# Four transposes, the weights and the outputs share three PSUM banks; the norm's guard moves in front of the logarithm

## The reference, cut to what matters

```python
def l2norm(t):
    return t / jnp.maximum(jnp.linalg.norm(t, axis=-1, keepdims=True), 1e-12)
...
q = l2norm(q) * qs
k = l2norm(k) * ksc
q = q * cos * scale + rotate_half(q) * sin * scale
k = k * cos * inv + rotate_half(k) * sin * inv
out = local_attention(q, k, v)          # each window sees itself and the window before it
return out.reshape(b, n, INNER) @ Wo
...
for i in range(DEPTH):                  # DEPTH = 6
    x = attn_layer(shift_tokens(x), ...) + x
    x = ffn_layer(shift_tokens(x), ...) + x
```

## Time and profile before

| | |
|---|---|
| median of 3 runs | 4022.69 us (4015.24 to 4051.56) |
| the profiled execution | 4047.98 us, its span 4046.1 us |
| busy in the span | PE 3125.7 us (77%), DVE 2893.7 (72%), ACT 2117.6 (52%), POOL 1116.3 (28%) |
| stretch of the six layers, 1847 to 4046 us | PE 1731.61, DVE 1592.81, ACT 1237.02, POOL 1031.53 us busy |
| mean TensorE clock granted there | 0.98 |
| stretch ahead of it, 0 to 1793 us | PE 1379.29, DVE 1271.36, ACT 871.76 us busy |

### The profile page before, as it was taken

How to read it: one execution, slowest core, us unless ns; L and a number is a source line. 1 busy time by engine, 2 the same in 40 slices (tenths; PEclk the granted TensorE clock), 3 DMA queues, 4 the chain that set the end, 5 groups by cost and what they waited for, 6 DMA issues and landing times. The chain is left out here.

```text
span 4046.1 us, 67071 instructions
## 1 busy us (share of the span) xinstructions
PE 3125.7 (77%) x25619; PEld 1597.3 (39%) x25853; DVE 2893.7 (72%) x4198; ACT 2117.6 (52%) x3147; POOL 1116.3 (28%) x627
## 2 busy tenths in 40 slices
PE   3899999994433888966777777777877777777887
PEld 1122222221321333324554555355545535554554
DVE  4888888875742788846775777677677767776775
ACT  2366666664221455654664565465556646654664
POOL 2000000000020000015553555355345535553551
PEclk7799999997666999988999999999999999999999
DMA  3200000000023000001111101000110011110100
GB/s 93 37 1 1 1 1 1 1 1 6 0 72 46 2 1 1 1 33 41 30 30 34 33 27 45 26 27 28 39 33 28 27 34 34 32 44 22 32 27 22
DMA packets 56649, 100.33 MB, mean 25 GB/s; under 512 B 19782, under 2 KB 38148, under 8 KB 54916
## 3 DMA queue, kind: packets, MB, share of 16 engines
q1 hardware_dynamic: 56324, 95.92, 9.2%
HBM read 37.95 MB, written 7.34 MB: 11 GB/s over the span
## 5 line engine op out<-in xcount | busy, mean ns | idle before, releaser
L456 DVE TENSOR_REDUCE a_part<-ps 128x1 f32<-128x512 f32 (+3 forms) x1664 | 1010.9, 656 | 343.3 <-PE ps L330 310.4
L440 ACT ACTIVATE a_Pb<-ps 128x1024 f32<-128x1024 f32 (+3 forms) x832 | 778.3, 973 | 640.6 <-PE ps L406 634.2
L1013 PE MATMUL ps<-l_w_qkv,l_XS 128*128 128x512 f32 x1152 | 586.0, 632 | 206.8 <-DVE l_weights L1403 163.0
L330 PE MATMUL ps<-a_KS,a_QS 128*128 128x512 bf16 (+3 forms) x1592 | 567.5, 385 | 102.4 <-DMA a_QS<-pieces 44.3
L956 POOL TENSOR_TENSOR l_sine<-l_qn,l_tab 128x512 f32<-128x512 f32 x192 | 341.4, 1778 | 776.8 <-DVE l_qn L1375 776.7
L406 PE MATMUL ps<-a_QS,a_KS 128*128 128x512 bf16 (+3 forms) x1598 | 466.9, 368 | 19.6 <-DVE a_part L456 7.1
L1362 DVE TENSOR_REDUCE l_norm<-l_square 128x8 f32<-128x512 f32 x384 | 262.0, 686 | 298.1 <-ACT l_square L1217 286.7
L383 PE MATMUL ps<-a_Pb,V 128*32 128x512 f32 (+3 forms) x3328 | 422.8, 580 | 2.6 <-ACT a_Pb L440 1.3
L330 PEld LDWEIGHTS ps<-a_KS,a_QS 128*128 128x128 bf16 x1664 | 145.2, 98 | 649.7 <-DVE a_part L456 573.1
L1024 PE MATMUL ps<-ident,l_hat 128*128 128x128 f32 x1536 | 252.0, 288 | 150.9 <-ACT l_kT L1241 67.2
L1013 PEld LDWEIGHTS ps<-l_w_qkv,l_XS 128*128 128x128 f32 x1152 | 206.5, 199 | 383.3 <-DVE l_weights L1403 175.5
(11 more groups left out here) (184 smaller groups left out, 4605.5 us busy)
## 6 DMA issues: line engine op xcount, KB each, us to landing
l_V_earlier<-l_V SPq DMA_DIRECT2D x96, 384.0 KB, 3.5
l_V_earlier<-l_V SPq DMA_DIRECT2D x96, 128.0 KB, 3.4
l_w_qkv<-in_L_ffn_Wqkv_dram SPq DMA_DIRECT2D x6, 1536.0 KB, 8.2
pieces<-a_piece SPq DMA_DIRECT2D x12, 512.0 KB, 2.6
a_KS<-pieces SPq DMA_DIRECT2D x48, 128.0 KB
a_QS<-pieces SPq DMA_DIRECT2D x48, 128.0 KB
l_w_o<-in_L_ffn_Wo_dram SPq DMA_DIRECT2D x6, 512.0 KB, 3.9
a_cos<-in_c_cos_dram SPq DMA_DIRECT2D x2, 1024.0 KB, 5.4
```

The source lines that it names most:

```text
L330: mm = e.matmul(bank[:, 0:width], QS[:, c, head, qt * P:(qt + 1) * P], KS[:, head, b * CH:b * CH + width], start=not masked, stop=True, sk ...
L440: e.activation(Pb[:, n % 2, 2 * p:2 * p + 2, a:CH], ps[:, 2 * p:2 * p + 2, a:CH], ACT.Exp)\
L456: e.tensor_reduce(part[:, u % 2, h * TC + qt, b:b + 1], ps[:, 4 + n % 2, 0:width], AX.X, ALU.max)\
L1013: e.matmul(ps[:, (V_BANK[T] if i == 2 else 0) + b, :], XS[:, T * P:(T + 1) * P], w_qkv[:, at:at + CH], start=True, stop=True).then_inc(s.a ...
```

## The change

The turned q and k groups no longer share one bank: r = 0 and 3 use bank 2, r = 1 bank 7, r = 2 bank 5. Bank 7 and bank 5 are those into which the values' outputs go, so turns 1 and 2 wait for `store_o` of two tiles ago, and turn 3 waits only for the copy of turn 0. The turned weights go into banks 7 and 5 and wait for the copies of turn 1 and turn 2 of the tile. Their wait for the residual goes; `out_project` takes it over. Bank 6 is `out_project`'s alone within a tile.

The clamp after the exponential goes. In its place, `sum_squares` writes its 16 sums beside 16 constants of `NORM_MIN ** 2` (`bounded`, set once by GpSimd) and takes the larger of each pair with one more reduction, in front of the logarithm; the added constant becomes 0. `project` and the banks of the projections are as they were.

```diff
--- before.py
+++ after.py
@@ -775,7 +775,6 @@
 ML = MI - (MT - 1) * P
 QK_SCALE = 8.0
 LN_RANGE = 2.0 ** 24
-LN_TINY = 2.0 ** -60
 NORM_MIN = 1e-12
 START = 1
 O_START = 4
@@ -790,10 +789,10 @@
 LN_EXP = "natural_log_exp_and_others"
 MEAN_BANK = [0, 1, 0, 6]
 VAR_BANK = [0, 1, 2, 7]
-TURN_BANK = 2
+TURN_BANK = [2, 7, 5, 2]
 SCORE_BANK = 3
 V_BANK = [0] + [SCORE_BANK] * (NT - 1)
-PT_BANK = [5, 6]
+PT_BANK = [7, 5]
 O_BANK = [7, 5]
 Y_BANK = 6
 SHIFTS = 4 * NC
@@ -821,7 +820,8 @@
         base = sb("base", [P, 4, NT, LD])
         tab = sb("tab", [P, 4, NT, LD])
         square = sb("square", [P, LH, LD])
-        norm = sb("norm", [P, 4, LH])
+        norm = sb("norm", [P, 3, LH])
+        bounded = sb("bounded", [P, LH, 2])
         qn = sb("qn", [P, 2, LH, LD])
         cosine = sb("cosine", [P, 2, LH, LD])
         sine = sb("sine", [P, LH, LD])
@@ -871,6 +871,7 @@
                     e.memset(wT[:, :, :, :], 0.0)
                     e.memset(V[:, :, :], 0.0)
                     e.memset(means[:, :], 1.0 / P)
+                    e.memset(bounded[:, :, :], NORM_MIN ** 2)
 
                 @block.tensor
                 def _(e):
@@ -1018,10 +1019,13 @@
                     n = l * NT + T
                     i = r // 2
                     e.wait_ge(s.rotated, START + (n * 2 + i) * 3 + 3)
-                    e.wait_ge(s.t_free, START + 4 * n + r)
+                    if r in (1, 2):
+                        e.wait_ge(s.o_free, START + (2 * n - 4 + r if T > 1 else l * (2 * NT)))
+                    else:
+                        e.wait_ge(s.t_free, START + 4 * n + (1 if r else 0))
                     for j in range(4):
                         at = (4 * (r % 2) + j) * P
-                        tr = e.transpose(ps[:, TURN_BANK, j * P:(j + 1) * P], hat[:, i, at:at + P], t.ident[:, :])
+                        tr = e.transpose(ps[:, TURN_BANK[r], j * P:(j + 1) * P], hat[:, i, at:at + P], t.ident[:, :])
                     tr.then_inc(s.t_ready, 1)
 
                 def scores(l, T, f):
@@ -1050,8 +1054,8 @@
                     if f == 0:
                         e.wait_ge(s.normed, n + 1)
                         e.wait_ge(s.o_free, START + 2 * n)
-                    else:
-                        e.wait_ge(s.added, START + n)
+                    if T + 1 < NT:
+                        e.wait_ge(s.t_free, START + 4 * (n + 1) + 2 + f)
                     for k in range(4):
                         j = 4 * f + k
                         tr = e.transpose(ps[:, PT_BANK[f], k * P:(k + 1) * P],
@@ -1080,6 +1084,7 @@
 
                     n = l * NT + T
                     e.wait_ge(s.o_free, START + 2 * n + 2)
+                    e.wait_ge(s.added, START + n)
                     if T == 0:
                         e.wait_ge(s.w_o, (l + 1) * 16)
                     for j in range(PAIRS):
@@ -1219,7 +1224,7 @@
 
                 def inverse_norms(l, T, i):
                     n = (l * NT + T) * 2 + i
-                    e.wait_ge(s.total, START + 2 * n + 2)
+                    e.wait_ge(s.bound, n + 1)
                     e.activation(norm[:, 1, :], norm[:, 0, :], ACT.Ln, bias=const[:, 0:1], scale=LN_RANGE).then_inc(s.root, 1)
                     e.wait_ge(s.root, 2 * n + 1)
                     e.activation(norm[:, 2, :], norm[:, 1, :], ACT.Exp, bias=const[:, 1:2], scale=-0.5).then_inc(s.root, 1)
@@ -1234,11 +1239,11 @@
                     e.wait_ge(s.t_ready, START + 4 * n + r + 1)
                     j0 = 4 * (r % 2)
                     if r < 2:
-                        bank = ps[:, TURN_BANK, :].rearrange("p (j w q) -> p j w q", j=4, q=WIN)
+                        bank = ps[:, TURN_BANK[r], :].rearrange("p (j w q) -> p j w q", j=4, q=WIN)
                         e.copy(qT[0:LD, T % 2, j0:j0 + 4, :, 0, :], bank[0:LD, :, :, :])
                         e.copy(qT[LD:P, T % 2, j0:j0 + 4, :, 1, :], bank[LD:P, :, :, :]).then_inc(s.t_free, 1)
                     else:
-                        e.copy(kT[:, T % 2, j0:j0 + 4, WIN:WIN + P], ps[:, TURN_BANK, :].rearrange("p (j n) -> p j n", j=4))\
+                        e.copy(kT[:, T % 2, j0:j0 + 4, WIN:WIN + P], ps[:, TURN_BANK[r], :].rearrange("p (j n) -> p j n", j=4))\
                             .then_inc(s.t_free, 1)
                     if r == 3 and T + 1 < NT:
                         e.wait_ge(s.t_free, START + 4 * n + 4)
@@ -1359,13 +1364,13 @@
                     for b in range(2):
                         heads = slice(HALF * b, HALF * (b + 1))
                         e.wait_ge(s.square, 2 * n + b + 1)
-                        e.tensor_reduce(norm[:, 0, heads], square[:, heads, :], AX.X, ALU.add).then_inc(s.total, 1)
+                        e.tensor_reduce(bounded[:, heads, 0], square[:, heads, :], AX.X, ALU.add).then_inc(s.total, 1)
+                    e.wait_ge(s.total, START + 2 * n + 2)
+                    e.tensor_reduce(norm[:, 0, :], bounded[:, :, :], AX.X, ALU.max).then_inc(s.bound, 1)
 
                 def normalise(l, T, i):
                     n = (l * NT + T) * 2 + i
                     e.wait_ge(s.root, 2 * n + 2)
-                    e.tensor_scalar(norm[:, 3, :], norm[:, 2, :], 1.0 / NORM_MIN, None, ALU.min).then_inc(s.bound, 1)
-                    e.wait_ge(s.bound, n + 1)
                     if T:
                         e.wait_ge(s.rotated, START + (n - 2) * 3 + (2 if i else 3))
                     else:
@@ -1373,7 +1378,7 @@
                     for b in range(2):
                         heads = slice(HALF * b, HALF * (b + 1))
                         e.tensor_tensor(qn[:, i, heads, :], ps[:, b, :].rearrange("p (h d) -> p h d", h=HALF),
-                                        norm[:, 3, heads].unsqueeze(2).to_broadcast([P, HALF, LD]), ALU.mult).then_inc(s.qn, 1)
+                                        norm[:, 2, heads].unsqueeze(2).to_broadcast([P, HALF, LD]), ALU.mult).then_inc(s.qn, 1)
 
                 def cosines(l, T, i):
                     n = (l * NT + T) * 2 + i
@@ -1564,7 +1569,7 @@
     low = lambda m: np.where(m, 0.0, -1e30)
     mask_c = np.stack([np.tile(low(seen), (1, 8)), np.tile(np.concatenate([low(seen0), low(seen)], 1), (1, 4))], 1)
     const = np.zeros((P, 4), np.float32)
-    const[:, 0], const[:, 1], const[:, 2] = LN_TINY, 0.5 * np.log(LN_RANGE), EPS
+    const[:, 0], const[:, 1], const[:, 2] = 0.0, 0.5 * np.log(LN_RANGE), EPS
     const[:, 3] = growth[i % LD] ** (CH // (WIN // 2))
     return {
         "c_base": base, "c_mask_c": mask_c.astype(bf16), "c_const": const,
```

## The result

The changed kernel takes **3881.06 us** (median of 4 runs, 3858.76 to 3883.05). The kernel before, run beside it, takes 4036.76 us (median of 4, 4015.24 to 4051.56); the ratio is 0.961, with a 95% interval of 0.954 to 0.967. The forecast was 3906 us, in a range of 3873 to 3995. The profiled executions stand at 3881.76 us and, before, at 4047.98 us; their spans are 166.1 us apart.

A forecast was written before the change was run, and what follows sets the result against it. VectorE ends each tile; its wait for k's squares was traced to two TensorE waits. Steady tiles 101, edges 12, tile 15 2 and start 1.5 sum to 117 us off a median of 4022.69: 3906 us, range 3873 to 3995.

The forecast's parts named there:

- The steady tile: The 78 tiles between a layer's edges: 1.3 us gained in each (bounds 1.1 and 1.5), 101 us in all.
- the hat: VectorE's addition of k's rotated halves: pushed by q's new reduction from 15.60 to 15.95.
- the added one: The new 32-element reduction for k ahead of the logarithm: 0.20 us, from 22.65 to 22.85, not held by GpSimd.
- both waits: TensorE's waits in a steady tile, turn 3 for turn 2's copy (0.68 us), second weights for the residual (0.73): both go.
- that rival: k's multiplication is held behind GpSimd's sum: only 0.25 us a tile gained, 3995 us; chance 0.08.
- the slower one: The added reduction is held behind GpSimd's sum like the clamp: 0.70 us a tile lost, 4077 us; chance 0.05.
- wait for `store_o`: Turns 1 and 2 wait for output copies stored some 6 us earlier: nothing; if one appeared, the forecast was wrong.
- half gain: Computed waits and the reduction's latency cost 0.3 us more on both halves: 0.65 us a tile, 3964 us; chance 0.08.
- The edges: Tiles 0 and 1 of each layer: 1.0 us gained in each, 12 us in all, between 4 and 15.
- tile 15: Each layer's last tile: some 1.8 us of the residual's wait goes, counted in the last layer alone; 2 us, at most 11.
- the stall: TensorE's 3.01 us stall in tile 15's values while w_qkv loads: as long as before, or longer by up to 1.8 us.
- the start: Start of the layers: one clamp held for 1.97 us goes, 1.5 us back.

The follow-up runs named there:

- scalar_max: The changed kernel with the guard in the same place as a tensor_scalar maximum with a constant instead of the added reduction: 4208.53 us, ratio 1.042.
- guard_only: The kernel before with the small reduction in front of the logarithm instead of the clamp, banks as before: 4003.94 us, ratio 0.994.
- banks_only: The changed kernel with the old clamp back behind the exponential and the added reduction gone: 4079.24 us, ratio 1.011.
- turns_only: The changed kernel with the turned weights back in banks 5 and 6 and waiting for the residual before their second group: 3968.05 us, ratio 0.980.
- late_load: The kernel before with the w_qkv load, ahead of the scales, held until tile 14's output copies are signalled: 4053.08 us, ratio 1.003.
- scales_first: The kernel before with the next layer's scales loaded first and w_qkv only behind tile 14's output copies: 4024.34 us, ratio 1.000.
- hat_early: The changed kernel with VectorE adding k's rotated halves before reducing the squares of the next tile's q: 3954.69 us, ratio 0.977.

## Why the prediction was right, and where it was off

**The steady tile** was read rightly, 1.39 us in the layer of the earlier trace rows for a forecast of 1.3. Counted from the first reduction, the forecast had the hat at 0.95, q's multiplication at 2.20, k's reductions at 6.33, the added one at 7.65 and k's multiplication at 8.60 to 8.70; they came at 1.02, 2.17, 6.27, 7.59 and 8.60. Over all 78 tiles it is 111.4 us for 101, inside the bounds of 86 to 117. The argument that both waits must go together, and the clamp with them, is borne out by the runs that leave one in (18.75, 18.37 and 20.19 us).

**The rivals.** k's multiplication starts at 2304.30, inside GpSimd's sum (2303.01 to 2305.38), with its duration unchanged: that rival has fallen. So has the slower one, for a `tensor_reduce`; scalar_max shows that it was one form of instruction away, and that its price was 4209 us and not 4077, since the sum for it had no term for the clock. No wait for `store_o` appears before L1028, and no half gain.

**The edges** were priced at 12 us and gave 23.8. Tile 1 gave 1.3 us each, near the 1.0 taken. Tile 0 gave 2.6 us, 15.8 in six layers. The moved guard alone gives 8.7 us of these (guard_only, 91.4 us from first hat to subtraction), the exchange of banks alone 0.9 (banks_only, 99.2). So more than half is the clamp and its hold, which I had priced from one row of tile 1; the rest needs both halves of the change, and most of it is the turns' banks (turns_only, 85.5).

**The step that failed is tile 15**: 2 us in the forecast, at most 11, and 25.4 us measured. The residual's wait fell from 2.67 to 0.71 us, about as said, and the tile gave 14.2 us in six layers (2.4 each; 1.8 were taken, and for the last layer alone). The residual of the first layer now:

```profile
2112.28 0.29 DVE L1431 TENSOR_TENSOR X<-X,ps 128x128 f32<-128x128 f32 x1 [0.71 <-PE ps L1091]
```

What was wrong is the sentence that set that gain off against the stall: "if that stall ends with the load, TensorE waits longer by what it arrives sooner". The stall does end with the load, but in the runs above it begins only where the fetch of instructions meets the load (but for 0.54 us once). The changed kernel fetches before it, so the stall is gone in all five layers: 11.2 us more. With both parts counted the sum would have been about 140 us and not 117.

Of the 49.7 us by which the sum (116.5) falls short of the timelines (166.2), tile 15 is 23.4, the edges 11.8, the steady tiles 10.4, the start, which is scatter, 3.5 and the end 0.6. That the forecast of 3906 us is only 25 us too high is in part luck: the gain between the medians was 156 us and not 117, 39 us more, but the 117 were taken off a median of 4022.69 us, 14 us lower than the 4036.76 us measured beside the changed kernel.

## What to carry to other kernels

Where two waits stand one behind the other ahead of the same piece of work, price them together: here one alone gave 0.38 us, the other nothing, and both 1.14 us. Before a short operation on VectorE moves in time, look at what GpSimd does then, and choose a form that isn't held: the same guard costs 0.19 us as a reduction and 2.12 us as a scalar operation. And look at how long TensorE stands idle ahead of its next work, and at the granted clock behind it: a reordering that gained 0.2 us a tile in one layer cost 1.1 us in the others, with the clock.

## What was not expected of the hardware

- **The granted clock within a tile.** Behind an idle time of TensorE of 2.71 us (hat_early), 3.26 (banks_only) and 3.60 (scalar_max) the six passes of the next projection took 4.22, 4.54 and 4.54 us, at a mean granted clock of 0.87 to 0.93 over 40 us; behind 1.68 us (changed kernel), 1.56 (turns_only) and 2.49 (last layer of hat_early) they took 2.84 us at 1.00. A single pass takes 0.59 us at the upper level (2.4 GHz) and up to 1.22 us in banks_only where the lower one (1.2 GHz) is granted, and only part of the passes behind the gap are that long. The idle time alone doesn't decide: in banks_only the third tile of each of the first five layers keeps 1.00 behind 3.27 us, and in its last layer, with 2.9 us of idle time in each tile, four tiles of thirteen keep it and nine fall to 0.91. What decides between them no run here isolates. Filling the idle time brought the clock back. The Trainium skill (TensorE: Matmul & The Clock Gate, "Part 1: The HAM clock gate") has the clock follow how busy TensorE has been; the traces agree.
- **A fetch of instructions held up by a load of weights.** By the packets' times, 16 KB of TensorE's program waited for a load of 1,536 KB, and TensorE with it, for up to 3.3 us; with the load issued later (late_load, scales_first) no stall over 0.54 us was left. Nothing on its own row but "issue" tells of it; the queue q8 in the DMA view does.
- **VectorE's copy and its operation of three operands held by GpSimd's tables**: 2.39 us for 0.42 and 2.71 us for 0.75, which took back what late_load had won.
